# A ternary feed-forward whose SiLU is one ScalarE activation instead of a sum, a tanh and a VectorE product

## The reference, cut to what matters

```python
h = bit_linear(x, w1)                       # 512 -> 2048, quantised rows of x, ternary w1
h = depthwise_conv1d(h.transpose(0, 2, 1), conv_w, conv_b)   # 3 taps along the positions, plus conv_b
h = h.transpose(0, 2, 1)
h = jax.nn.silu(h)
return bit_linear(h, w2)                    # 2048 -> 512, quantised again by the row's largest |h|
```

## Time and profile before

| | |
|---|---|
| median of three runs | 2224.13 us (2219.16 to 2231.52) |
| profiled execution | 2225.15 us, its span 2223.4 us |
| mean granted TensorE clock | 0.944 of full speed |
| busy: PE, DVE, ACT, POOL | 88%, 67%, 43%, 54% |
| `bit_ffn` | about 750 to 1104 us; turns 1 to 6 take 37.4 us each |

### The profile page before, as it was taken

The page is one execution under the profiler, slowest core; times in us unless marked ns, Lnnn a source line. Parts: engine busy times, 40 slices in busy tenths (PEclk is TensorE's granted clock), DMA queues, the critical chain, the costliest instruction groups (busy, mean ns, idle before and its releaser), DMA issues. The chain is left out here.

```text
span 2223.4 us, 42254 instructions
## 1 busy us (share of the span) xinstructions
PE 1949.8 (88%) x15208; PEld 1376.2 (62%) x15208; DVE 1488.3 (67%) x2752; ACT 948.1 (43%) x1289; POOL 1201.5 (54%) x1470
## 2 busy tenths in 40 slices
PE   5798898898897478989678999999999977899997
PEld 3466676676676377777445666666666664455553
DVE  4776776776765479898444666666666546898973
ACT  3276666666667573333132434344344443111111
POOL 4175766766655453232321467577576422787763
PEclk9899999999997589999888999999999988999998
DMA  7454444344330321111163344444444521011100
GB/s 205 103 128 110 103 121 118 103 115 119 101 95 22 126 75 34 41 33 33 53 196 93 92 133 145 126 133 145 136 131 129 178 62 38 24 33 38 33 24 29
DMA packets 184011, 208.67 MB, mean 94 GB/s; under 512 B 61480, under 2 KB 145704, under 8 KB 183336
## 3 DMA queue, kind: packets, MB, share of 16 engines
q1 hardware_dynamic: 183848, 206.46, 32.8%
HBM read 138.61 MB, written 67.53 MB: 93 GB/s over the span
## 5 line engine op out<-in xcount | busy, mean ns | idle before, releaser
L709 POOL TENSOR_TENSOR a_p_hl<-a_p,a_p_hl 125x448 bf16<-125x448 f32 x540 | 564.9, 1048 | 500.9 <-ACT a_p_hl L842 472.7
L1008 DVE TENSOR_REDUCE a_nm<-a_psum 112x1 f32<-112x750 f32 x256 | 237.3, 934 | 127.7 <-PE a_psum L1262 126.2
L832 ACT ACTIVATE a_p<-a_psum 125x1344 f32<-125x1344 f32 x192 | 247.8, 1291 | 149.2 <-PE a_psum L1242 137.9
L842 ACT ACTIVATE a_p_hl<-a_p 125x1344 bf16<-125x1344 f32 x192 | 254.1, 1323 | 97.3 <-PE a_psum L1280 93.3
L1280 PEld LDWEIGHTS a_psum<-a_v_st,a_p_hl 125*128 125x128 bf16 x4608 | 179.9, 99 | 39.4 <-issue 18.9
L1280 PE MATMUL a_psum<-a_v_st,a_p_hl 125*128 125x65 bf16 (+2 forms) x4608 | 191.3, 196 | 10.3 <-POOL a_p_hl L709 4.1
L1913 PE MATMUL f_conv<-f_u,f_taps 128*128 128x224 f32 x768 | 161.3, 360 | 22.3 <-DVE f_u L1765 21.4
L1152 PE MATMUL a_psum<-a_chl,a_w 128*128 128x375 bf16 x768 | 147.2, 339 | 30.9 <-DVE a_w L899 15.5
L1262 PE MATMUL a_psum<-a_k_st,a_q_st 96*112 96x375 bf16 x512 | 131.1, 343 | 42.3 <-DVE a_nm L1008 25.1
L1913 PEld LDWEIGHTS f_conv<-f_u,f_taps 128*128 128x128 f32 x768 | 141.7, 191 | 31.8 <-DVE f_u L1765 27.1
L1152 PE MATMUL a_psum<-a_chl,kept_w 128*128 128x375 bf16 x768 | 137.5, 332 | 23.8 <-DVE kept_w L899 17.9
(11 more groups left out here) (251 smaller groups left out, 4057.8 us busy)
## 6 DMA issues: line engine op xcount, KB each, us to landing
a_k<-a_k_tmp SPq DMA_DIRECT2D x64, 375.0 KB, 3.0
a_k_st<-a_k SPq DMA_DIRECT2D x96, 187.5 KB, 3.3
kept_k<-a_k SPq DMA_DIRECT2D x96, 187.5 KB, 3.4
a_c<-in_ctx_t SPq DMA_DIRECT2D x16, 750.0 KB, 5.8
ctx_parts<-a_chl SPq DMA_DIRECT2D x16, 750.0 KB, 9.6
a_chl<-ctx_parts SPq DMA_DIRECT2D x16, 750.0 KB, 6.1
a_q_st<-a_q SPq DMA_DIRECT2D x192, 56.0 KB, 2.2
rounded<-a_fw SPq DMA_DIRECT2D x24, 352.0 KB, 3.8
```

What stands on the lines that cost most here:

```text
L709: ins = nc.gpsimd.tensor_tensor(p_hl[0:MC, h % 2, 1, cols], p32[0:MC, h % 2, cols], p_hl[0:MC, h % 2, 0, cols], ALU.subtract)
L832: nc.scalar.activation(p32[0:MC, par, :].rearrange("p (b n) -> p b n", b=3), st[0:MC, :, 0:2 * S], ACT.Exp, scale=scale).then_inc(exp_done, 1)
L842: nc.scalar.activation(p_hl[0:MC, par, 0, :], p32[0:MC, par, :], ACT.Copy).then_inc(phi_done, 1)
L1008: ins = nc.vector.tensor_reduce(out, sm_[0:HALF, 0:2, 0:MK], AX.XY, ALU.max, negate=True)
```

## The change

ScalarE reads the convolution's bank once per chunk and writes h itself, with the function Silu and the bias cb. The tiles t, th and cb_half, the semaphore th_ready and VectorE's `finish_group` are gone. h_ready is now counted by ScalarE, and TensorE and the maxima over h wait on it. Before the first group of a turn ScalarE waits until h of two rows ago has been rounded (hq_ready, given an offset of two so that the wait is never on zero). h is silu itself, no longer twice that, so the two constants change.

```diff
@@ -1350,7 +1350,6 @@
     FC = F // P
     GC = 2
     NG = FC // GC
-    RING = 4
     W = F * D // P
 
     with ExitStack() as ctx:
@@ -1397,10 +1396,7 @@
         sB = sb("sB", [P, S], F32)
         u = sb("u", [P, 2, GC, S + 2], F32)
         taps = sb("taps", [P, FC, 3, P], F32)
-        cb_half = sb("cb_half", [P, FC], F32)
         round_sb = sb("round", [P, 2], F32)
-        t = sb("t", [P, RING, GC, S], F32)
-        th = sb("th", [P, RING, GC, S], F32)
         h = sb("h", [P, 2, FC, S], F32)
         hm = sb("hm", [P, 3, S], F32)
         hqT = sb("hqT", [P, FC, S], BF16)
@@ -1424,8 +1420,8 @@
             sem("w2_rounded"), sem("w2_ready"), sem("act_own"), sem("cw_in"), sem("abs_ready"), sem("act_taps"))
         xn_ready, xq_ready, xT_ready, xqT_ready, dB_mm, dB_ready = (
             sem("xn_ready"), sem("xq_ready"), sem("xT_ready"), sem("xqT_ready"), sem("dB_mm"), sem("dB_ready"))
-        up_ready, u_ready, conv_ready, th_ready, h_ready = (
-            sem("up_ready"), sem("u_ready"), sem("conv_ready"), sem("th_ready"), sem("h_ready"))
+        up_ready, u_ready, conv_ready, h_ready = (
+            sem("up_ready"), sem("u_ready"), sem("conv_ready"), sem("h_ready"))
         taps_ready, dq_ready = sem("taps_ready"), sem("dq_ready")
         hm_ready, hmT_ready, hinv_ready, sB_mm, sB_ready = (
             sem("hm_ready"), sem("hmT_ready"), sem("hinv_ready"), sem("sB_mm"), sem("sB_ready"))
@@ -1613,7 +1609,6 @@
                 absolute_sum(0, q, w1q)
             act.wait_ge(small_in, 32)
             nc.scalar.activation(tg[:, :], g_sb[:, :], ACT.Tanh).then_inc(gate_ready, 1)
-            nc.scalar.activation(cb_half[:, :], cb[:, :], ACT.Copy, scale=0.5).then_inc(gate_ready, 1)
 
             def prepare(b):
 
@@ -1634,17 +1629,15 @@
                         quantise_w1(ACT_W1[g + 1])
                     if first and 2 <= g < 6:
                         absolute_sum(1, g - 2, w2q)
-                    if not (isinstance(b, int) and n < RING):
-
-                        act.wait_ge(h_ready, n - RING + 1)
+                    if g == 0 and not (isinstance(b, int) and b < 2):
+
+                        act.wait_ge(hq_ready, b * 2)
                     act.wait_ge(conv_ready, n + 1)
                     for c in range(GC):
                         ch = g * GC + c
-                        src = conv[:, g % 2, c * S:(c + 1) * S]
-                        nc.scalar.activation(t[:, g % RING, c, :], src, ACT.Identity, bias=cb[:, ch:ch + 1])
-                        ins = nc.scalar.activation(th[:, g % RING, c, :], src, ACT.Tanh, scale=0.5,
-                                                   bias=cb_half[:, ch:ch + 1])
-                    ins.then_inc(th_ready, 1)
+                        ins = nc.scalar.activation(h[:, par, ch, :], conv[:, g % 2, c * S:(c + 1) * S], ACT.Silu,
+                                                   bias=cb[:, ch:ch + 1])
+                    ins.then_inc(h_ready, 1)
                     if g == 0 and in_range(b - 1):
                         row_scales(b - 1)
                 if not in_range(b):
@@ -1673,7 +1666,6 @@
             act.wait_ge(dB_mm, 1)
             nc.scalar.activation(dB[:, :], dB_ps[:, 0:S], ACT.Copy).then_inc(dB_ready, 1)
             quantise_w1(ACT_W1[1])
-            act.wait_ge(gate_ready, 2)
             turns(act.Fori, turn)
 
         @block.vector
@@ -1748,12 +1740,6 @@
             dve.wait_ge(scale_ready, 1)
             link(nc.vector.tensor_scalar(w_mean[:, 0:1], w_mean[:, 0:1], 1.0 / 127.0, None, ALU.mult))
 
-            def finish_group(b, par, g):
-
-                dve.wait_ge(th_ready, b * NG + g + 1)
-                nc.vector.scalar_tensor_tensor(h[:, par, g * GC:(g + 1) * GC, :], th[:, g % RING, :, :], 1.0,
-                                               t[:, g % RING, :, :], ALU.add, ALU.mult).then_inc(h_ready, 1)
-
             def group(b, g):
 
                 n = b * NG + g
@@ -1771,7 +1757,7 @@
                 dve.wait_ge(hmT_ready, b + 1)
                 link(nc.vector.tensor_reduce(hmax[:, :], hmT_ps[0:HALF, 0:2 * P].rearrange(
                     "p (s u) -> p s u", s=2), AX.X, ALU.max))
-                link(nc.vector.tensor_scalar(hmax[:, :], hmax[:, :], 2e-5, None, ALU.max))
+                link(nc.vector.tensor_scalar(hmax[:, :], hmax[:, :], 1e-5, None, ALU.max))
                 link(nc.vector.reciprocal(hinv[:, :], hmax[:, :]))
                 link(nc.vector.tensor_scalar(hinv[:, :], hinv[:, :], 127.0, None, ALU.mult))
                 for s in range(2):
@@ -1807,8 +1793,6 @@
                 for g in range(NG):
                     if in_range(b):
                         group(b, g)
-                        if g >= 2:
-                            finish_group(b, par, g - 2)
                     if in_range(b - 1):
                         if g == 0:
                             row_scales(b - 1)
@@ -1829,7 +1813,7 @@
                             mean_and_scale(1)
                             dve.wait_ge(gate_ready, 1)
                             dve.wait_ge(scale_ready, 2)
-                            link(nc.vector.tensor_scalar(w_mean[:, 1:2], w_mean[:, 1:2], tg[:, 0:1], 0.5 / 127.0,
+                            link(nc.vector.tensor_scalar(w_mean[:, 1:2], w_mean[:, 1:2], tg[:, 0:1], 1.0 / 127.0,
                                                          ALU.mult, ALU.mult))
                     if g >= NG - 2 and in_range(b):
                         at, quarter = g - (NG - 2), QH // 2
@@ -1837,8 +1821,6 @@
                     if g == NG - 1 and in_range(b):
                         link(nc.vector.tensor_tensor(hm[:, 0, :], hm[:, 0, :], hm[:, 1, :], ALU.max))
                 if in_range(b):
-                    finish_group(b, par, NG - 2)
-                    finish_group(b, par, NG - 1)
                     link(row_maxima(b, par, 2, QH, FC))
                     nc.vector.tensor_tensor(hm[:, 0, :], hm[:, 0, :], hm[:, 2, :], ALU.max).then_inc(hm_ready, 1)
                 if in_range(b - 1):
@@ -1847,6 +1829,7 @@
             row_factors()
             quantise_w1(0)
             quantise_w1(2)
+            dve.sem_inc(hq_ready, 2)
             turns(dve.Fori, turn, lambda i: own.enter_loop(i, 2 * FFN0_LINKS),
                   lambda: own.leave_loop((B - 2) // 2))
 
@@ -1901,7 +1884,7 @@
                 n = b * NG + g
 
                 if not (isinstance(b, int) and n < 2):
-                    pe.wait_ge(th_ready, n - 1)
+                    pe.wait_ge(h_ready, n - 1)
                 if isinstance(b, int) and b == 0:
                     if (g + 1) * GC <= POOL_TAPS:
                         pe.wait_ge(act_taps, 1)
@@ -1937,7 +1920,7 @@
                         for c in range(FC):
                             if s == 0 and c % QH == 0:
 
-                                pe.wait_ge(hq_ready, (b - 1) * 2 + c // QH + 1)
+                                pe.wait_ge(hq_ready, b * 2 + c // QH + 1)
                             ins = nc.tensor.matmul(down[0:HALF, s, :], hqT[:, c, s * HALF:(s + 1) * HALF],
                                                    w2q[:, c, :], start=(c == 0), stop=(c == FC - 1))
                         ins.then_inc(down_ready, 1)
```

## The result

| | before | after |
|---|---|---|
| median | 2228.6 us (2219.16 to 2235.0, 10 runs) | 2210.74 us (2205.75 to 2217.18, 10 runs) |
| ratio | | 0.9927, 95% interval [0.9907, 0.9947] |
| profiled execution, span | 2225.15, 2223.4 us | 2217.18, 2215.4 us |

The kernel is 0.73% faster, about 16 us; the interval allows 12 to 21. I had forecast 7.7 us. The time lies in the range that I gave, 2206 to 2229, but well under its middle, and the outcome is "faster by more than 0.5%", to which I gave 0.30; "within 0.5%" had 0.57. The gain is about twice the one that I summed.

What follows compares the result with a forecast made beforehand. TensorE was taken as the bound, waiting for u from VectorE, which GpSimd's products block. Turns 1 to 6 (4.9 us) plus turn 0 (2.8) gave 7.7 us: 2216.5 us on the median, range 2206 to 2229.

Steps and rivals of the forecast that it cites:

- Turns 1 to 6: Ternary feed-forward: u(5) and group 5's convolution come 0.82 us earlier per turn, 4.9 us over six turns (0 to 12.6).
- the first diag: VectorE, before u(5): two diag tensor_scalars now fall inside GpSimd's burst, each held by a product; u(5) at 879.05, not 879.87.
- The next convolutions follow without a gap: Turn 2 before the change: TensorE has no wait behind group 5's convolution, so nothing is gained after u(5).
- the other five turns repeat this within 0.1 us: Turns 1 to 6: turn 2's gaps (0.78, 1.70, 0.67 us before groups 3, 4, 5) recur, period 37.4 us.
- Turn 0: First turn, no down projection: the transposes of the maxima start 2.5 to 3.1 us earlier, 2.8 taken.
- Both causes named: Turn 0: u(7) no longer behind ScalarE's late absolute sums (0.9 us), and a shorter finish from conv 7 to the transposes.
- The clock at the end of turn 0: Idle stretch before the transposes: they might precede the clock's fall to 1.2 GHz, saving 1.6 us; not summed.
- The tail: Turn 8 (row scales, GpSimd's product, down projection): no edited instruction, 0 us.
- B: TensorE bound all through: diag operations pass GpSimd (12.6), turn 0 gives 2.8, clock holds (1.6): 17.0 us, 2207.1; 22%.
- A: The outcome as summed, 7.7 us gained: 2216.5 us; 45%.
- C: Gain eaten: u(5) bound by the end of GpSimd's burst, only turn 0 pays: 2.8 us, 2221.3; 13%.
- D: Slower: tables reloaded in ScalarE's loops, 18 loads of 1.28 us, 23 us; 2239.5 all exposed, 2228 half exposed; 17%.

Runs made afterwards that it cites:

- run 1: Changed kernel with VectorE again doing one product of two SBUF inputs per group, into a scratch tile: ratio to before 1.0002, period of turns 2 to 6 37.44 us.
- run 4: Changed kernel with VectorE's extra product only behind u(3) and u(4), inside GpSimd's burst of eight products: period 37.06 us.
- run 7: Changed kernel with GpSimd's eight products h times sB cut to 4 of 224 columns: period 33.15 us.
- run 8: Kernel before, with GpSimd's eight products h times sB cut to 4 of 224 columns: period 33.15 us.
- run 5: Changed kernel with VectorE's extra product only behind u(6), outside GpSimd's burst: period 35.96 us against 35.94.
- run 6: Changed kernel with VectorE's extra products behind u(5) and u(6), outside GpSimd's burst: period 36.33 us.
- run 2: Changed kernel with a second ScalarE ACTIVATE (Identity, into a scratch tile) before each Silu: ratio to before 0.994, period 35.96 us, turn 0 40.0 us.
- run 3: Changed kernel with the second ACTIVATE (Identity, into a scratch tile) behind each Silu: ratio to before 0.9949, period 35.96 us, turn 0 35.8 us.
- run 10: Changed kernel with VectorE's preparation of the next row one group later and the first maxima over h behind u(7): ratio to before 0.9892, median 2201.1 us.
- run 11: Kernel before, without Silu, with VectorE's preparation one group later and the first maxima over h later: ratio 0.9943, period 35.76 us.

## Why the prediction was right in its mechanism and short in its sum

1. *What bounds.* TensorE waiting for u(4) and u(5) behind VectorE, and VectorE in steps of GpSimd's products: runs 1, 4, 7 and 8 show it. The Trainium skill's rule (SBUF — State Buffer, Who interferes with whom), by which VectorE in a two-port mode and GpSimd exclude each other for a whole instruction, agrees with the two cut kernels: 0.17 us for the 112x2 tensor_scalar that took 0.94 in the earlier trace rows.
2. *Turns 1 to 6, the mis-sized term: 0.82 a turn forecast, 1.53 measured (4.9 against 9.5 us).* Two parts. (i) Up to u(5) it was 1.12. The steps came as retimed, up to the first diag, which lost its turn to GpSimd; I let the second lose too, and it did not (0.27 us). That is 0.3. (ii) "The next convolutions follow without a gap", read in the kernel before, was wrong, and so nothing was summed behind u(5): u(7) was late there and cost 0.4 us. That stands on the weight loads and not on the matmul rows that I read, and runs 5 and 6 show that it takes two products to bring it back. Nor did "the other five turns repeat this within 0.1 us" hold: turn 1 took 38.79 us and had 0.11 us, not 0.78, before conv 3.
3. *Turn 0: 2.8 forecast, 3.5 measured.* Up to conv 3 the turn scatters by microseconds from kernel to kernel (conv 3 starts 14.0 to 19.5 us after the first up projection), by when row 1's x lands and by the clock (run 2). In the two kernels compared x landed alike, the moments starting 7.45 and 7.48 us after the first up projection: luck, without which the 3.5 would not have been so clean. Of the 3.5, 0.3 lie between conv 2 and conv 3, where u(3) was late before; the prediction had nothing there. From conv 3 to the transposes it is 3.2 (22.6 to 19.4), and that holds: runs 4, 5, 6 and 7 took 19.4 there too. Both causes named are there: up to conv 7, behind the sums, 1.2 (12.81 to 11.65; 0.9 forecast), and from there, the shorter finish, 2.0 (9.77 to 7.74; 1.9 forecast).
4. *The clock at the end of turn 0* was not in the sum, rightly: in the kernel after, the transposes came after 4.33 us of waiting instead of 6.37, and the clock fell just then. The 16 up projections still took 3.19 us. But the clock came back sooner: 3.7 to 4.5 us behind the transposes it was 0.50 before (824.0 to 824.8 us) and 1.00 after (830.8 to 831.6), and turn 1 reached conv 3 0.3 us earlier. With these 0.3 turn 1 gained 1.9, the others 1.5.
5. *The tail: 0 forecast, 2.1 measured, and not the change's.* The second half of the last down projection took 7.43 us before, 5.39 after: the clock came back sooner; why it did is not shown. That half begins at 1093.79 before and at 1091.11 after; the stretch 1096 to 1097 before, still at 0.50, and 1091 to 1092 after, already at 1.00:

```profile
1096.00:1097.00 1.00, 1.00 (x4) 0.58 (x3) 0.00 (x0) 0.00 (x0) 0.00 (x0) 0.50 0.00 0
```

```profile
1091.00:1092.00 1.00, 0.89 (x4) 0.57 (x5) 0.06 (x1) 0.00 (x0) 0.00 (x0) 1.00 0.00 0
```

   The tail takes about 20.4 or 22 to 22.4 us in most other kernels as well: 20.35 with the products back, 22.04 with one of them.
6. *Rivals.* B's 17.0 us is nearer to the measured 16 than the 7.7 of A, but by luck: one diag did pass GpSimd, yet its 2.1 a turn needs u(4) and u(5) both in time, and conv 5 still waits 1.0; its 1.6 for the clock did not come, and the tail's 2.1 stood in no rival. C is out: the gain was not eaten. D is out twice: two loads more, not eighteen, both in idle time, and even 127 loads in this stage left the period as it was.

Added up, 13.0 us of the profile's 15.0 are the change's, 9.5 in turns 1 to 6 (0.3 of it by the clock) and 3.5 in turn 0; the runs' 16 us agree within the interval. The same comparison holds for the other five kernels that were run several times: the stage is 0.9, 9.6, 11.9, 24.9 and 12.2 us shorter than before in runs 1, 2, 3, 10 and 11, and the ratios give 0, 13, 11, 24 and 13, each within its interval.

## What to carry to other kernels

When VectorE and GpSimd work side by side, an operation's price on VectorE is not its duration but what it does to the order in which the two take turns: count in steps of the longer instruction, and note that one product outside the burst was free and two cost 0.4 us a turn, while two inside it cost 1.1. Read TensorE's weight loads for gaps as well as its matmuls. An activation function of another table cost nothing where its load stood ahead of a wait, and TensorE nothing in run 2 either, where it stood behind one: the result that it held up was not the one that TensorE waited for. When a row names what ended a wait, check in the program that the engine waits for just that instruction.

## What was not expected of the hardware

- With 127 table loads of 1.28 us in the stage turns 2 to 6 were no longer than with one, though ScalarE needed 3.6 us a group against TensorE's 3.06.
- A u that came late cost what the weight loads stood idle, 2.76 us a turn in the kernel after, and not the 2.0 that the matmuls show.
- The same tail, from the last transposes on, took 20.36 us after and 22.41 before, by when the granted clock came back from 1.2 to 2.4 GHz, in kernels that do the same there.
- The same program ahead of the stage ended almost 18 us apart (775.5 to 793.1 us), more than the whole effect. What moves it stays open; no run here was made for it. The three kernels made from the one before lie at 775.5 to 782.1 us and the eleven with Silu at 779.0 to 793.1. That looks like a shift by the change, but the medians above leave little room for one: with the products back (run 1) they agree with the stage's 0.9 us to within 3.
